# Half of layer 0's routing moved into attention's last unit, and the last layer's expert weights made TensorE's stationary operand

## The reference, cut to what matters

```python
x = x + attn0(layernorm(x)) ; x = x + moe0(layernorm(x))
x = x + attn1(layernorm(x)) ; x = x + moe1(layernorm(x))

# attn0: 16 heads of 16. softmax(k k^T, strictly lower) * beta + I = A;
u = solve_triangular(A, v, lower=True)
o = softmax(causal(q k^T)) @ u ; attn0 = o @ Wo
# moe0: 64 experts of 96, top 8, at most C = 256 tokens an expert, in token order
logits = x @ gate_w.T ; probs = softmax(logits) ; scores, idx = top_k(probs, 8)
xbuf = zeros((E, C, D)).at[e_sorted, pos].set(x[tok_sorted], mode='drop')
y = einsum(silu(xbuf @ w_gate.T) * (xbuf @ w_up.T), w_down)
out = zeros.at[tok_sorted].add(y[e_sorted, pos] * score * valid)
# attn1: elu features, cumsum over positions of phi_k * v, times phi_q, @ Wo
# moe1: 8 experts of 512, top 2, weights renormalised
h = silu(x @ w1[e].T) * (x @ w3[e].T) ; out += combine[:, e] * (h @ w2[e].T)
```

## Time and profile before

| | us |
|---|---|
| median of 3 runs | 1074.27 (1070.15 to 1076.11) |
| the profiled execution, its own time | 1068.96 |
| its span, from the first to the last instruction | 1067.1 |
| PE busy, share of the span | 717.5 (67%) |
| DVE busy | 563.0 (53%) |
| ACT busy | 309.9 (29%) |
| POOL busy | 251.4 (24%) |

### The profile page before, as it was taken

One profiled execution on the slowest core, in us unless ns is written; L12 is line 12 of the kernel. 1 busy time (PEld: TensorE's weight loads), 2 busy tenths in 40 slices (PEclk: granted clock), 3 DMA queues, 4 the chain that ended last, 5 costly groups with the idle time before them and its releaser, 6 DMA issues. The chain is left out here.

```text
span 1067.1 us, 16859 instructions
## 1 busy us (share of the span) xinstructions
PE 717.5 (67%) x6126; PEld 525.6 (49%) x6127; DVE 563.0 (53%) x1659; ACT 309.9 (29%) x530; POOL 251.4 (24%) x258
## 2 busy tenths in 40 slices
PE   4957287777857758760211999999605264599995
PEld 2433274354445437450111999999504253266663
DVE  5986985996799592248100333333246286233332
ACT  1014234443551544420000344444104243111110
POOL 5002102111120210003774000000667604122222
PEclk9989698978979975975555999999756676699998
DMA  3871005223340971029833788888523203132220
GB/s 129 163 99 36 1 3 179 40 33 63 128 61 2 384 274 51 1 70 353 336 131 122 266 287 290 291 290 292 157 61 94 84 0 103 52 50 45 40 35 1
DMA packets 72951, 135.97 MB, mean 127 GB/s; under 512 B 12464, under 2 KB 35504, under 8 KB 71856
## 3 DMA queue, kind: packets, MB, share of 16 engines
q1 hardware_dynamic: 58304, 100.15, 31.3%
q0 software_dynamic: 10224, 21.12, 7.4%
q10 hardware_dynamic: 4352, 13.77, 3.4%
HBM read 75.28 MB, written 60.43 MB: 127 GB/s over the span
## 5 line engine op out<-in xcount | busy, mean ns | idle before, releaser
L1152 PE MATMUL scores<-wgu,zero 128*128 128x192 f32 x512 | 97.8, 336 | 9.7 <-issue 8.9
L1253 DVE TENSOR_TENSOR val<-sel,scores 128x192 f32<-128x192 f32 x64 | 22.7, 354 | 152.9 <-ACT sel L1295 95.4
L655 DVE TENSOR_REDUCE block_maxima<-scores 128x10 f32<-128x1280 f32 x64 | 92.3, 1486 | 8.0 <-PE scores L354 7.0
L850 ACT ACTIVATE E<-scores 128x1280 f32<-128x1280 f32 x64 | 77.5, 1237 | 58.4 <-PE scores L365 32.4
L1152 PEld LDWEIGHTS scores<-wgu,zero 128*128 128x128 f32 x512 | 85.2, 197 | 10.6 <-issue 9.3
L1309 POOL DMA_INDIRECT expert_rows<-xn_moe,scatter_slots x64 | 62.6, 978 | 115.0 <-DVE gather_slots L1229 95.8
L1567 PE MATMUL scores<-w,xgT 128*128 x184 | 87.8, 601 | 0.3 <-issue 0.3
L1169 PE MATMUL scores<-wd,slot 96*128 96x256 f32 x256 | 68.9, 393 | 10.9 <-issue 9.1
L962 POOL TENSOR_SCALAR_AFFINE_SELECT E<-E 128x256 f32<-128x256 f32 x64 | 27.2, 449 | 208.2 <-ACT E L850 208.1
L1286 ACT COPY zero<-misc 128x512 f32<-128x512 f32 x64 | 37.5, 586 | 116.3 <-PE misc L1145 56.5
L1145 PE MATMUL misc<-cf,xg 128*128 128x128 f32 x256 | 40.6, 282 | 40.0 <-issue 38.9
...
...
## 6 DMA issues: line engine op xcount, KB each, us to landing
...
```

What stands on the lines that cost most here:

```text
L655: nc.vector.tensor_reduce(bm[:, c, h, :], scores[:, slot, 0:WIDE].rearrange("p (a n) -> p a n", n=P), AX.X, ALU.max).then_inc(s_fd, 1)
L850: nc.scalar.activation(to[:, h, :], scores[:, k % 2, 0:WIDE], ACT.Exp, scale=SCALE).then_inc(s_fa, 1)
L1152: ins = nc.tensor.matmul(scores[:, j % 2, t * 2 * F0:(t + 1) * 2 * F0], xgT[:, j % 2, k, t * P:(t + 1) * P], wgu[:, j // GE, j % GE, k, :] ...
```

## The change

- **First sequence early.** `first_sequence` on TensorE, VectorE and ScalarE puts the first sequence's output projection, residual sum, norm, logits, softmax, selection and ranks into the eight join steps of the last unit, where the next unit's row scores stood for the earlier ones. The transposes of its attention output come at the end of unit 2. `slots_first` puts its slots and 32 weight picks into the four steps of the last `solve`. Its tiles live in the score stacks of unit 2, which are free by then; SyncE loads `wo0`, a second copy of x and the gate weights there, behind a wait for unit 2's exponentials and ahead of the 22 zero-fills.
- **Scatters.** GpSimd issues the first 12 of the first sequence's 32 scatters at the end of the attention block (`EARLY`), the other 20 at the beginning of the next, and then, after the second sequence's slots, its 32. An expert needs 4 scatters of a level of the second sequence instead of 8 of both.
- What stands after the last unit and in the next block now covers four tiles (`T1_`) instead of eight.
- The constants `cf` are loaded in four pieces, two of them into `bankT` and `bankD`; ScalarE's first copy into `bankD` waits for the last split part.
- **Last layer.** `project` has the weights stationary and the rows moving, 128 columns at a time, so that the hidden rows come out turned; `turn_h` and `copy_h` are gone. `w13` has four slots instead of eight experts; SyncE loads the expert's 1 MB for each of the 23 tiles, four tiles ahead. `w2` stays resident.

```diff
+EARLY = 12
...
+def turn_second(pe, n, src):
+  for p in range(HT // 2):
+    for k in range(KT):
+      for t in range(2):
+        c = (2 * k + t) * P
+        ins = nc.tensor.transpose(misc[:, p, c:c + P], src[:, HT + 2 * p + t, k * P:(k + 1) * P], identf)
+    ins.then_inc(s_tr, 1)
+def copy_second(act, n):
+  for p in range(HT // 2):
+    act.wait_ge(s_tr, n + p + 1)
+    nc.scalar.copy(xnT[:, :, T + 2 * P * p:T + 2 * P * (p + 1)],
+           misc[:, p, :].rearrange("p (k n) -> p k n", k=KT)).then_inc(s_xnT, 1)
...
+def scatter(pool, k, t, rows):
+  pool.indirect_dma_start(
+    out=xbuf, out_offset=bass.IndirectOffsetOnAxis(ap=isc[:, t, k:k + 1], axis=0),
+    in_=rows, in_offset=None, bounds_check=E0 * CAP - 1,
+    oob_is_err=False).then_inc(s_gb[k], 16)
...
+  cosT, sinT = bankT[:], bankD[:]
...
+  free = {c: stk[c][:, 0].rearrange("p h n -> p (h n)").bitcast(F32) for c in ("k", "B", "q")}
...
+  xT0 = free["k"][:, 0:KT * T].rearrange("p (k n) -> p k n", k=KT)
+  X0 = tiles_of("k", KT * T, D)
+  xn0 = tiles_of("q", 0, D)
+  wo0 = free["q"][:, HT * D:HT * D + KT * D].rearrange("p (k n) -> p k n", k=KT)
+  pr0, sel0, val0, slot0, Vg0, Vs0 = [tiles_of("B", HT * E0 * i, E0) for i in range(6)]
+  pick0 = free["B"][:, HT * E0 * 6:HT * E0 * 6 + 8 * E0].rearrange("p (j n) -> p j n", j=8)
+  s_ev, s_x0, s_pk0 = sem("ranks_read"), sem("x0_copied"), sem("weight_picked0")
...
+      def turn_first(n, src):
+        for p in range(HT // 2):
+          for k in range(KT):
+            for t in range(2):
+              c = T + (2 * k + t) * P
+              ins = nc.tensor.transpose(scores[:, p, c:c + P],
+                           src[:, 2 * p + t, k * P:(k + 1) * P], identf)
+          ins.then_inc(s_tr, 1)
+      def first_sequence(q):
+        if q in (0, 1):
+          if q == 0:
+            pe.wait_ge(s_xnT, 6)
+            pe.wait_ge(s_wol, 16)
+          for t in (2 * q, 2 * q + 1):
+            for k in range(KT):
+              ins = nc.tensor.matmul(scores[:, q, 2 * T + (t % 2) * D:2 * T + (t % 2 + 1) * D],
+                         xT0[:, k, t * P:(t + 1) * P], wo0[:, k, :],
+                         start=(k == 0), stop=(k == KT - 1))
+            ins.then_inc(s_wo, 1)
+        if q == 4:
+          pe.wait_ge(s_xn, NT + HT)
+          turn_first(6, xn0)
+        if q == 5:
+          pe.wait_ge(s_xnT, 8)
+          pe.wait_ge(s_gw, 16)
+          for t in T0:
+            for k in range(KT):
+              ins = nc.tensor.matmul(scores[:, 0, t * E0:(t + 1) * E0], xT0[:, k, t * P:(t + 1) * P],
+                         gate0[:, k, :], start=(k == 0), stop=(k == KT - 1))
+          ins.then_inc(s_lg, 1)
+        if q == 7:
+          pe.wait_ge(s_sel, 1)
+          for t in T0:
+            for p in range(t + 1):
+              ins = nc.tensor.matmul(scores[:, 1, t * E0:(t + 1) * E0], triu if p == t else onesb,
+                         selb[:, p, :], start=(p == 0), stop=(p == t))
+          ins.then_inc(s_rk, 1)
...
+          else:
+            first_sequence(q)
         join(u, 7)
+        if last:
+          pe.wait_ge(s_ev, 1)
...
-      pe_transposes(pe, 1, AO, lambda p: pe.wait_ge(s_ao, 2 * UNITS))
-      pe.wait_ge(s_xnT, 8)
-      pe.wait_ge(s_wol, 16)
-      for t in range(NT):
...
+        if u == UNITS - 2:
+          pe.wait_ge(s_ao, UNITS)
+          turn_first(4, AO)
+      pe.wait_ge(s_ao, 2 * UNITS)
+      turn_second(pe, 8, AO)
+      pe.wait_ge(s_xnT, 10)
+      for t in T1_:
+        pe.wait_ge(s_xw, t - 1 if t > HT + 1 else HT)
...
+          if u + 1 == UNITS:
+            slots_first(it)
...
+      def first_sequence(q):
+        if q in (1, 2):
+          if q == 1:
+            dve.wait_ge(s_x, 32)
+          for t in (2 * q - 2, 2 * q - 1):
+            dve.wait_ge(s_wo, t + 1)
+            nc.vector.tensor_tensor(X0[:, t, :], scores[:, q - 1, 2 * T + (t % 2) * D:2 * T + (t % 2 + 1) * D],
+                        X0[:, t, :], ALU.add).then_inc(s_xw, 1)
+        if q == 2:
+          dve.wait_ge(s_xw, HT)
+          dve_norm(dve, link, 1, xn0, T0, X0)
+        if q == 6:
+          dve.wait_ge(s_lg, 1)
+          link(nc.vector.tensor_reduce(mx0, lg0, AX.X, ALU.max))
+          nc.vector.tensor_tensor(pr0, lg0, mx0.unsqueeze(2).to_broadcast(b0), ALU.subtract).then_inc(s_sub, 1)
+        if q == 7:
+          dve.wait_ge(s_ex, 1)
+          link(nc.vector.tensor_reduce(mx0, pr0, AX.X, ALU.add))
+          link(nc.vector.reciprocal(mx0, mx0))
+          link(nc.vector.tensor_tensor(pr0, pr0, mx0.unsqueeze(2).to_broadcast(b0), ALU.mult))
+          for t in T0:
+            ins = nc.vector.max(m8[:, t, :], pr0[:, t, :])
+          link(ins)
+          for t in T0:
+            ins = nc.vector.match_replace(sel0[:, t, :], m8[:, t, :], pr0[:, t, :], -1.0)
+          link(ins)
+          nc.vector.tensor_scalar(selb[:, 0:HT], sel0, 0.0, None, ALU.is_lt).then_inc(s_sel, 1)
+      def read_ranks():
+        dve.wait_ge(s_rk, 1)
+        link(nc.vector.tensor_scalar(slot0, rk0, float(CAP), -1.0, ALU.min, ALU.add))
+        link(nc.vector.tensor_scalar(val0, rk0, float(CAP), None, ALU.is_le))
+        nc.vector.sem_inc(s_ev, 1)
...
+      def slots_first(it):
+        if it == 0:
+          link(nc.vector.tensor_tensor(slot0, slot0, base0.unsqueeze(1).to_broadcast(b0), ALU.add))
+          link(nc.vector.tensor_scalar(slot0, slot0, -1.0, BIG, ALU.mult, ALU.add))
+          link(nc.vector.tensor_tensor(Vg0, slot0, selb[:, 0:HT], ALU.mult))
+        if it == 1:
+          link(nc.vector.tensor_tensor(Vs0, Vg0, val0, ALU.mult))
+          for t in T0:
+            nc.vector.max(V8s[:, t, :], Vs0[:, t, :])
+            ins = nc.vector.max(V8g[:, t, :], Vg0[:, t, :])
+          link(ins)
+          nc.vector.tensor_scalar(isc[:, 0:HT], V8s[:, 0:HT], -1.0, BIG, ALU.mult, ALU.add).then_inc(s_idx, 1)
+          nc.vector.tensor_scalar(ig[:, 0:HT], V8g[:, 0:HT], -1.0, BIG, ALU.mult, ALU.add).then_inc(s_idx, 1)
+        if it == 2:
+          link(nc.vector.tensor_tensor(pr0, pr0, val0, ALU.mult))
+        if it >= 2:
+          for g in range(16 * (it - 2), 16 * (it - 1)):
+            t, k = g // K0, g % K0
+            if g >= 8:
+              dve.wait_ge(s_pk0, g - 7)
+            nc.vector.scalar_tensor_tensor(
+              out=pick0[:, g % 8, :], in0=Vg0[:, t, :], scalar=V8g[:, t, k:k + 1], in1=pr0[:, t, :],
+              op0=ALU.is_equal, op1=ALU.mult, accum_out=w8[:, t, k:k + 1]).then_inc(s_pk0, 1)
...
+          else:
+            first_sequence(q)
+        if last:
+          read_ranks()
...
+        if u == 0:
+          act.wait_ge(s_parts, 8)
...
+      def first_sequence(q):
+        if q == 2:
+          act_std(act, 1, T0)
+        if q == 4:
+          copy_first(6)
+        if q == 6:
+          act.wait_ge(s_sub, 1)
+          nc.scalar.activation(pr0, pr0, ACT.Exp).then_inc(s_ex, 1)
+        if q == 7:
+          act.wait_ge(s_xw, HT)
+          act.wait_ge(s_tt, 8 * UNITS)
+          nc.scalar.copy(X[:, 0:HT, :], X0).then_inc(s_x0, 1)
...
+          if u + 1 == UNITS:
+            first_sequence(q)
...
+        if u == UNITS - 2:
+          copy_first(4)
+      copy_second(act, 8)
...
+      pool.wait_ge(s_idx, 2)
+      pool.wait_ge(s_zf, 16 * NZ)
+      for g in range(EARLY):
+        scatter(pool, g // HT, g % HT, xn0[:, g % HT, :])
...
-      sp.dma_start(cf[:], a["cf"][:, 0:CF]).then_inc(s_w, 16)
+      sp.dma_start(cf[:, 0:P], a["cf"][:, 0:P]).then_inc(s_w, 16)
+      sp.dma_start(cf[:, P:CF - 1024], a["cf"][:, P + 1024:CF]).then_inc(s_w, 16)
+      sp.dma_start(cosT, a["cf"][:, P:P + 512]).then_inc(s_w, 16)
+      sp.dma_start(sinT, a["cf"][:, P + 512:P + 1024]).then_inc(s_w, 16)
...
+      sp.wait_ge(s_fa, use(1, UNITS - 2) + GH)
+      sp.dma_start(wo0, a["wo0"].rearrange("(k p) n -> p k n", p=P)).then_inc(s_wol, 16)
+      sp.dma_start(X0, a["x"][0:T].rearrange("(t p) d -> p t d", p=P)).then_inc(s_x, 16)
+      sp.dma_start(gate0[:], a["gate0"].rearrange("(k p) n -> p k n", p=P)).then_inc(s_gw, 16)
       for z in range(NZ1):
...
       sp.wait_ge(s_tt, 8 * UNITS)
-      sp.dma_start(wo0, a["wo0"].rearrange("(k p) n -> p k n", p=P)).then_inc(s_wol, 16)
-      sp.dma_start(X[:], a["x"].rearrange("(t p) d -> p t d", p=P)).then_inc(s_x, 16)
-w13 = sb("w13", [P, E1, KT, 2 * F1])
+      sp.dma_start(X[:, HT:NT, :], a["x"][T:N].rearrange("(t p) d -> p t d", p=P)).then_inc(s_x, 16)
...
+w13 = sb("w13", [P, 4, KT, 2 * F1])
...
+      for t in T1_:
         for k in range(KT):
...
-      pe.wait_ge(s_sel, 1)
-      for t in range(NT):
+      pe.wait_ge(s_sel, 2)
+      for t in T1_:
...
-        act.dma_start(w13[:, e], a["w13"][e].rearrange("p (k n) -> p k n", k=KT)).then_inc(s_w1, 16)
         act.dma_start(w2[:, e], a["w2"][e].rearrange("p (k n) -> p k n", k=FT)).then_inc(s_w1, 16)
...
-      pool.wait_ge(s_idx, 2)
-      pool.wait_ge(s_zf, 16 * NZ)
+      for g in range(EARLY, HT * K0):
+        scatter(pool, g // HT, g % HT, xn0[:, g % HT, :])
+      pool.wait_ge(s_idx, 4)
```

(49 more changed lines are left out.)

177 lines of the change are left out of this document (89 added, 88 removed).

## The result

The changed kernel takes 1064.79 us (median of 20 runs, 1058.32 to 1069.05) against 1073.47 us (20 runs, 1064.71 to 1078.38): a ratio of 0.9919, 95% interval 0.9901 to 0.9938. So it is faster by 8.7 us; 24.6 were forecast. The time lies in the range of the prediction, 15 us above its likeliest value. The profiled execution took 1064.41 us, its span is 1062.7. The profiled execution of before lay 4.5 us under its median, that of after 0.4 under, so the two profiles differ by 4.5 us only, where the medians differ by 8.7.

A forecast was written before the change was run, and what follows sets the result against it. GpSimd's issue of layer 0's scatters was taken as the bound. Terms 0.5 - 30.8 + 1.5 + 4 - 7.0 + 5.7 + 1.5 = -24.6 us, taken from the median 1074.27, gave 1049.7 us; range 1033 to 1070.

The forecast's parts named there:

- What bounds the kernel: Layer 0's scatter of expert rows, 494.1 to 577.0 us: GpSimd's issue is the bound, one indirect DMA every 1.28 us.
- Part 2: Last layer with weights stationary: -7.0 us in the tiles, +5.7 at the start, +1.5 for accumulating scatters; about zero.
- The rival of a layer bound by them: Last layer: each accumulating scatter waits behind a whole weight load, 7.0 us a tile; total 1081 us, chance 0.10.
- adding load to product: Last layer, TensorE: if weight load and product times added, a tile takes 8.8 us and the layer 69 us more.
- Removed work: Serial routing chain, 450.5 to 494.1 us: only the second sequence is left, 17.1 us less, 4.8 before the block's end.
- The join steps: Attention's last unit: the first sequence's routing put into its joins adds 15 us (bounds 6 and 24).
- The solve: Attention's last unit: the first sequence's slots and weight picks put into its solve add 7.5 us (5 to 9).
- The outputs: Attention outputs behind the last solve: forecast to change by 0 us.
- The late hand-overs: Results one engine signals to another, taken up late beside indirect DMA streams: +4 us, from none to two of 13.7.
- The first rival: Last unit: all insertions in series at half clock (24 + 9 us), a 13.7 us late signal in the solve; 1070, chance 0.15.
- signs of being wrong: Expert pace not within 10 us of last scatter, "remote" waits in solve or routing, tile above 5.8, last unit over 33 longer.
- The term of the linear stage: Stretch from layer 0's last down projection to the last layer's owners, with the gathers: forecast to change by 0 us.

The follow-up runs named there:

- without holds: The changed kernel itself, on a chip where no engine took up another's result late, against the kernel before there: 1018.90 us, ratio 0.98.

## Why the prediction was wrong

**What bounds the kernel**: right. GpSimd's issue was the bound of the stretch; without holds the 20 scatters start with the block (490.4) and the last of the 52 ends at 557.2, 1.28 us each, as the prediction had it.

**Part 2**: right in its sum, 1.0005, with two terms off that cancel: 5.53 us a tile (5.50), the first projection 7.3 and 7.5 us later behind the owners (5.7), the accumulating scatters landing in 3.8 us and hidden (nothing for +1.5). The rival of a layer bound by them is refuted here. So is adding load to product: the next instruction on TensorE starts 3.58 us behind the first of 32 passes (936.80 - 933.22), 0.112 each, where the forecast was 0.111 and the sum 0.2145. What the Trainium skill, DMA: Bandwidth & Descriptors, section "SWDGE vs HWDGE vs iDMA", says of a DMA engine going round-robin between its queues agrees with the landing, 3.8 us beside 1 MB loads and 3.7 without.

**Removed work**: right. To the block's start -4.8 as forecast, and -11.3 to the second slots without holds (-12.3).

**The join steps** were mis-sized, +21.5 for 15; this is the second step that failed. Step by step: projection and residual 3.7 (4 in the prediction), the normalisation 4.7 (3), transposes and logits 7.7 (4), the softmax and ranks 5.3 (5). The third is the miss. VectorE waited 7.85 us for the sums behind the logits: these stood behind ScalarE's two copies and then took 3.68 us at half clock, both in series with the step. I had priced them partly into idle time. Nor did the clock help as I had assumed: it was 0.57 over the joins instead of 0.50, but 0.50 from 417.0 to their end, where most of the added time lies; raising it did not shorten the joins. The misses by step are read from the trace and not undone by a run of their own.

**The solve**: 9.1 for 7.5 without holds. Of these the picks are 8.4 (forecast 6.4 in steps 2 and 3, at an unchanged clock). The outputs, costed at nothing, take 2.6 us more without holds, and 8.5 - 6.7 = 1.8 with the picks moved as well; that rest is not taken apart.

**The late hand-overs** are the step that failed most. "From none to two of 13.7 us; I take one short one, +4" put them into the sum as bad luck of a known size. On a chip that has them they come in every profile: in every profile of such a chip with an unbroken stream beside the second routing, the ranks were held until 4 to 6 us after its last issue (waits of 14.17, 14.23, 14.21, 12.84 and 14.21 us with 20 scatters, 31.62 and 30.74 with 32). Against the profile without them they cost the solve 36.4 - 30.4 = 6.0 us and the routing 33.2 - 20.9 = 12.3. GpSimd's own queue of scatters would have lost 4.6 of that anyway (45.9 us from the second slots to the last scatter without holds, 41.3 with them). So, counted from the end of the last unit's inverses, the last scatter came 173.8 - 159.8 = 14.0 us later than without them. Forecast there was -30.8 us, measured -6.0: of the 24.8 that are missing, 14.0 are the holds and 10.5 the joins, the solve and the outputs. The +4 should have been 14. The trace of before did show it, had I asked what would be critical in the stream: beside its own scatters two hand-overs had waited 33.5 us in sum, and a third stood between them:

```profile
553.54 0.59 ACT L1286 COPY zero<-misc 128x512 f32<-128x512 f32 x1 [10.17 <-remote]
```

They did not move its scatters, which were GpSimd's own pace (82.7 us, and 82.6 without holds), but on that chip the experts behind them also took 192.1 us, and 176.3 on the one without holds, so they were hardly free. That stage had them before and after the change; what the change added is held hand-overs where GpSimd itself waits for the result. On a chip without holds the median difference is 20.4 us of 1039.3, where the forecast without its 4 us for them would have been 28.6; the 8.2 us missing there are within the 10.5 above.

The first rival ("the last unit swallows the gain") came nearest: it had 33 us for joins and solve and one hand-over of 13.7 in the solve. Measured were 36.5 with 6.0 of holds in them, and another 12.3 in the routing, which it did not have. That the two profiles differ by 4.5 us where it said 4.4 is partly luck; the medians differ by 8.7. It was given 0.15. Two of the signs of being wrong that the prediction named did show: "remote" waits in the solve and the routing, and a last unit longer by over 33 us.

The term of the linear stage, forecast at zero, is +3.8 in the profiles: beside the gathers ScalarE's copy waited 18.74 us instead of 13.72. It looks like the same thing, with a size that differs from run to run (11.8 to 20.3 us in the profiles of chips that hold).
